# Last attention: scores and maxima contracted over one head's 32 rows, one head per row group

## The reference, cut to what matters

```python
x = x + _L1_attn_b_ref(_layernorm(x), W_qkv, b_qkv, W_o, b_o)

def _L1_attn_b_ref(x, W_qkv, b_qkv, W_o, b_o):        # 16 heads of 8, S = 1024
    Q, K, V = split(x @ W_qkv.T + b_qkv)              # each b, s, head, 8
    scores = einsum('bqhd,bkhd->bhqk', Q, K)
    scores = where(tril(ones(S, S)), scores, -inf)
    probs = softmax(scores / sqrt(8), axis=-1)
    return einsum('bkhd,bhqk->bqhd', V, probs).reshape(b, s, 128) @ W_o.T + b_o
```

## Time and profile before

| | us |
|---|---|
| three runs | 2196.89, 2202.60, 2202.69 |
| median | 2202.6 |
| span of the profiled execution | 2195.9 |
| last attention in it (1284 to 1959) | 675 |
| of this, units 1 to 14 (1372 to 1929.5) | 557.5, or 39.8 a unit |

### The profile page before, as it was taken

One profiled execution on the slowest core, in us unless ns is written; L12 is line 12 of the kernel. 1 busy time (PEld: TensorE's weight loads), 2 busy tenths in 40 slices (PEclk: granted clock), 3 DMA queues, 4 the chain that ended last, 5 costly groups with the idle time before them and its releaser, 6 DMA issues. The chain is left out here.

```text
span 2195.9 us, 35701 instructions
## 1 busy us (share of the span) xinstructions
PE 1937.5 (88%) x12178; PEld 1438.1 (65%) x12178; DVE 1695.5 (77%) x5509; ACT 1035.0 (47%) x1617; POOL 492.2 (22%) x558
## 2 busy tenths in 40 slices
PE   5886799998999967673799979999999999989999
PEld 3554699986899923332799965555555555549998
DVE  6997788876888879998688877766767767738887
ACT  3442244433444434442444444666666665554443
POOL 1110100012000022230200024534544543330000
PEclk8998999999999988876899989999999999999999
DMA  3000100000000010000000000000000000000000
GB/s 100 6 5 4 56 1 1 1 1 1 1 1 1 1 40 1 0 1 0 1 1 1 1 1 1 1 1 1 1 1 1 1 1 1 1 1 11 11 9 13
DMA packets 17638, 15.73 MB, mean 7 GB/s; under 512 B 4209, under 2 KB 16177, under 8 KB 16946
## 3 DMA queue, kind: packets, MB, share of 16 engines
q1 hardware_dynamic: 15152, 12.66, 1.8%
q10 hardware_dynamic: 2306, 0.78, 0.2%
HBM read 10.55 MB, written 2.88 MB: 6 GB/s over the span
## 5 line engine op out<-in xcount | busy, mean ns | idle before, releaser
L2205 ACT ACTIVATE soft_prob<-psum 128x1024 f32<-128x1024 f32 (+3 forms) x384 | 302.4, 812 | 203.8 <-PE psum L2085 202.2
L2297 DVE TENSOR_REDUCE soft_mx<-psum 128x1 f32<-128x512 f32 (+2 forms) x352 | 231.0, 688 | 116.1 <-PE psum L2155 79.3
L2155 PE MATMUL psum<-soft_own,soft_stack 128*128 128x512 f32 (+3 forms) x768 | 249.3, 376 | 24.5 <-DVE soft_mx L2293 10.7
L163 POOL TENSOR_TENSOR norm_rstd<-norm_mv,s_const_minus_half 128x4 f32<-128x4 f32 x64 | 65.2, 1019 | 915.0 <-DVE norm_mv L158 908.4
L2085 PE MATMUL psum<-soft_stack,soft_own 128*128 128x512 f32 (+3 forms) x768 | 225.4, 377 | 2.8 <-POOL soft_stack L2062 2.2
L2085 PEld LDWEIGHTS psum<-soft_stack,soft_own 128*128 128x128 f32 x768 | 125.3, 189 | 133.2 <-issue 81.6
L2293 DVE CUSTOM_DVE_ANT_0 psum<-psum,s_soft_sel 128x384 f32<-128x384 f32 (+1 forms) x256 | 157.4, 639 | 64.8 <-PE psum L2155 64.0
L2155 PEld LDWEIGHTS psum<-soft_own,soft_stack 128*128 128x128 f32 x768 | 139.8, 193 | 92.7 <-DVE soft_mx L2297 42.9
L1075 DVE SCALAR_TENSOR_TENSOR x<-psum,ffn1b_cw,x 128x128 f32<-128x128 f32 x512 | 144.1, 344 | 29.7 <-PE psum L949 20.9
L2102 PE MATMUL psum<-soft_prob,soft_v_pad 128*32 128x512 f32 (+3 forms) x1536 | 163.6, 498 | 3.5 <-ACT soft_prob L2205 2.1
L1075 DVE SCALAR_TENSOR_TENSOR x<-psum,ffn1a_cw,x 128x128 f32<-128x128 f32 x512 | 144.2, 344 | 27.2 <-PE psum L949 18.1
(11 more groups left out here) (381 smaller groups left out, 4114.0 us busy)
## 6 DMA issues: line engine op xcount, KB each, us to landing
s_ffn_w<-in_ffn_w SPq DMA_DIRECT2D x4, 1024.0 KB, 7.8
out_x<-x SPq DMA_DIRECT2D x8, 256.0 KB, 2.3
x<-in_x SPq DMA_DIRECT2D x4, 384.0 KB, 8.0
mamba_coef_dram<-mamba_out_coef SPq DMA_DIRECT2D x8, 96.0 KB, 1.6
s_ret_w<-in_ret_w SPq DMA_DIRECT2D x1, 640.0 KB, 3.5
x<-in_x SPq DMA_DIRECT2D x4, 128.0 KB, 3.5
s_ret_cos<-in_ret_cos SPq DMA_DIRECT2D x1, 512.0 KB, 7.0
s_ret_sin<-in_ret_sin SPq DMA_DIRECT2D x1, 512.0 KB, 7.3
```

Source lines behind the costliest of these rows:

```text
L163: self.nc.gpsimd.tensor_tensor(self.rstd[:, :], self.mv[:, :, 1], self.const["minus_half"][:, 0:GT], ALU.pow).then_inc(self.rstd_ready, 1)
L2155: ins = pe.matmul(per_head[:, n, :], stack[:, u % HT, i * P:(i + 1) * P], own[:, u % 3, g, half * BLK:half * BLK + width], start=(n == 0), ...
L2205: nc.scalar.activation(prob[:, done % PROBS, :, low(n):BLK], e_ps[:, n % 2, :, low(n):BLK], ACT.Exp, scale=float(HD) ** -0.5).then_inc(exp ...
L2297: nc.vector.tensor_reduce(mx[:, i, half, heads.start:heads.stop], bank[:, 0:width * len(heads)].rearrange("p (g k) -> p g k", k=width), AX ...
```

## The change

Scores and maxima contract over one head's 32 partitions and name their row group by `tile_position=(32 * g, 0)`. The masked copies `own`, their events, `ident` and `causal` are gone, and `keys` is kept for four units instead of two. A maxima job is always one head: 48 jobs a unit, and DVE adds the mask in all blocks of the diagonal (widths 128 to 512). Jobs come two per step, heads 2 and 3 in even steps and 0 and 1 in odd ones, where the scores of the step are of heads 0 and 1, and 2 and 3.

```diff
 def max_jobs():
         for half in range(1 + i // GT):
             width = min(BLK, (i + 1) * P - half * BLK)
-            heads = BLK // width
-            jobs += [(i, half, width, range(g, g + heads)) for g in range(0, HT, heads)]
+            jobs += [(i, half, width, g) for g in (2, 3, 0, 1)]
...
-            slots = [n for n in range(E_STEPS) for _ in range(2 if n % 2 or n % 8 == 0 else 1)]
             for j in range(M_JOBS):
-                at[slots[j * len(slots) // M_JOBS]].append(("m", u + 1, j))
+                at[j * E_STEPS // M_JOBS].append(("m", u + 1, j))
...
-            put((9, ("own", u + 2, 0)), (16, ("own", u + 2, 1)))
...
+        def head(g):
+            return slice(VW * g, VW * (g + 1))
...
 def scores(u, n):
                 for j in range(2):
-                    ins = pe.matmul(e_ps[:, n % 2, j, low(n):BLK], own[:, u % 3, 2 * pair + j, kt * P:(kt + 1) * P],
-                                    stack[:, u % HT, qb * BLK + low(n):(qb + 1) * BLK], start=True, stop=True)
+                    g = 2 * pair + j
+                    ins = pe.matmul(e_ps[:, n % 2, j, low(n):BLK], keys[head(g), u % HT, kt * P:(kt + 1) * P],
+                                    stack[head(g), u % HT, qb * BLK + low(n):(qb + 1) * BLK], start=True, stop=True,
+                                    tile_position=(VW * g, 0))
...
 kind == "m", PE
-                    for n, g in enumerate(heads):
-                        ins = pe.matmul(per_head[:, n, :], stack[:, u % HT, i * P:(i + 1) * P], own[...], ...)
-                    if half == i // GT and len(heads) > 1:
-                        ins = pe.matmul(per_head[:, :, width - P:width], ident[:, :], causal[...], ...)
-                    ins.then_inc(m_ready, 1)
+                    pe.matmul(bank[:, 0:width], stack[head(g), u % HT, i * P:(i + 1) * P],
+                              keys[head(g), u % HT, half * BLK:half * BLK + width], start=True, stop=True,
+                              tile_position=(VW * g, 0)).then_inc(m_ready, 1)
...
 kind == "st", ACT
-                    if i == 0 and b > 0:
+                    if b > 0:
                         act.wait_ge(score_ready, E_STEPS * (u - HT + 1))
-                    if i == 1 and u >= 2:
-                        act.wait_ge(*((own_first, 2) if u == 2 else (own_ready, 2 * (u - 2))))
...
 kind == "m", DVE
-                    if half == i // GT and len(heads) == 1:
+                    if half == i // GT:
                         nc.vector.tensor_tensor_reduce(bank[:, 0:width], bank[:, 0:width], mask_row[:, BLK - width:BLK],
-                                                       ..., mx[:, i, half, heads.start:heads.stop]).then_inc(m_done, 1)
+                                                       ..., mx[:, i, half, g:g + 1]).then_inc(m_done, 1)
                     else:
-                        nc.vector.tensor_reduce(mx[:, i, half, heads.start:heads.stop], bank[...] per head, AX.X, ALU.max)
+                        nc.vector.tensor_reduce(mx[:, i, half, g:g + 1], bank[:, 0:width], AX.X, ALU.max)
```

More of the change, by code:

```diff
@@ L1858, in softmax_events @@
     start = [("pad", 0), ("stat", 1), ("scale", 1), ("qk", 0, 1), ("qk", 0, 0)]
-    start += [first[0], ("own", 0, 0), ("v", 0), first[1]]
+    start += [first[0], ("v", 0), first[1]]
     start += [("xt", 1)] + maxima(0, 4) + [("qk", 1, 1)] + maxima(4, 8) + [("qk", 1, 0)] + maxima(8, M_FIRST)
-    start += [first[2], ("v", 1), second[0], ("sh", 0, 0), first[3], ("own", 0, 1)]
+    start += [first[2], ("v", 1), second[0], ("sh", 0, 0), first[3]]
     units = []
@@ L1877, in softmax_events @@
                 at[FIRST_STEPS + (j - 6) * (E_STEPS - FIRST_STEPS) // (M_JOBS - 6)].append(("m", 1, j))
-            put(*zip((1, 3, 4), second[1:]), (1, ("own", 1, 0)), (4, ("own", 1, 1)))
+            put(*zip((1, 3, 4), second[1:]))
             put((5, ("bias", 0)), (6, ("bias", 1)))
             put((9, ("oev", 0, 0)), *zip((10, 11, 13, 14), stack_events(0, 2)), (12, ("otr", 0, 0)), (15, ("sh", 1, 0)),
-                (12, ("own", 2, 0)), (16, ("own", 2, 1)), *zip((17, 18, 20, 21), stack_events(0, 3)), (19, ("pad", 1)))
+                *zip((17, 18, 20, 21), stack_events(0, 3)), (19, ("pad", 1)))
             units.append(at)
@@ L1908, in softmax_events @@
             put(*zip((15, 18), output_events(b)[0:2]))
-        if u + 2 < UNITS:
-            put((9, ("own", u + 2, 0)), (16, ("own", u + 2, 1)))
         units.append(at)
@@ L1936, in softmax_stage @@
         sel = sb("sel", [P, HT, 2, 2, P], F32R)
-        ident = sb("ident", [P, P], F32R)
-        causal = sb("causal", [P, P], F32R)
         full = sb("full", [P, BLK])
@@ L1941, in softmax_stage @@
         stack = sb("stack", [P, HT, SEQ], F32R)
-        keys = sb("keys", [P, 2, SEQ], F32R)
+        keys = sb("keys", [P, HT, SEQ], F32R)
         v_pad = sb("v_pad", [P, 2, TPB, HEADS, VW])
         prob = sb("prob", [P, PROBS, 2, BLK])
-        own = sb("own", [P, 3, HT, SEQ], F32R)
         mx = sb("mx", [P, TPB, 2, HT])
@@ L1955, in softmax_stage @@
         mask_ready = sem("mask_ready")
-        own_first, own_ready, top_ready = sem("own_first"), sem("own_ready"), sem("top_ready")
+        top_ready = sem("top_ready")
         sel_ready, pads_set, ones_set = sem("sel_ready"), sem("pads_set"), sem("ones_set")
@@ L2036, in event @@
                         nc.gpsimd.tensor_copy(mask_row[:, BLK - P:BLK], w["causal"][:, :]).then_inc(mask_ready, 1)
[L2037 to L2043, removed]
                 if kind == "stat":
@@ L2143, in event @@
                     u, j = at
-                    i, half, width, heads = MJOBS[j]
+                    i, half, width, g = MJOBS[j]
                     bank, back = m_bank(u, j)
                     if j in (0, M_FIRST):
-                        p = int(j > 0)
                         for part in range(2):
-                            pe.wait_ge(*freed("st", *divmod(u, HT), part, p))
-                        pe.wait_ge(*((own_first, p + 1) if u == 0 else (own_ready, 2 * (u - 1) + p + 1)))
+                            pe.wait_ge(*freed("st", *divmod(u, HT), part, int(j > 0)))
                     if M_JOBS * u + j >= back:
                         pe.wait_ge(m_done, M_JOBS * u + j + 1 - back)
-                    per_head = bank[:, 0:width * len(heads)].rearrange("p (g k) -> p g k", k=width)
-                    for n, g in enumerate(heads):
-                        ins = pe.matmul(per_head[:, n, :], stack[:, u % HT, i * P:(i + 1) * P],
-                                        own[:, u % 3, g, half * BLK:half * BLK + width],
-                                        start=(n == 0), stop=half != i // GT or len(heads) == 1)
-                    if half == i // GT and len(heads) > 1:
-                        ins = pe.matmul(per_head[:, :, width - P:width], ident[:, :],
-                                        causal[:, :].unsqueeze(1).to_broadcast([P, len(heads), P]),
-                                        start=False, stop=True)
-                    ins.then_inc(m_ready, 1)
+                    pe.matmul(bank[:, 0:width], stack[head(g), u % HT, i * P:(i + 1) * P],
+                              keys[head(g), u % HT, half * BLK:half * BLK + width], start=True, stop=True,
+                              tile_position=(VW * g, 0)).then_inc(m_ready, 1)
                 if kind == "sh":
@@ L2193, in _ @@
             act.wait_ge(*loaded)
-            nc.scalar.copy(ident[:, :], const["ident"][:, :])
-            nc.scalar.copy(causal[:, :], w["causal"][:, :])
             for t in range(HT):
@@ L2223, in event @@
                     u, now = HT * b + t, slice(p * BLK, (p + 1) * BLK)
-                    if i == 0 and b > 0:
+                    if b > 0:
                         act.wait_ge(score_ready, E_STEPS * (u - HT + 1))
-                    if i == 1 and u >= 2:
-                        act.wait_ge(*((own_first, 2) if u == 2 else (own_ready, 2 * (u - 2))))
-                    nc.scalar.activation(stack[:, t, now] if i == 0 else keys[:, u % 2, now], ps[:, :, :], ACT.Identity,
+                    nc.scalar.activation((stack if i == 0 else keys)[:, t, now], ps[:, :, :], ACT.Identity,
                                          bias=w["shift_rows"][:, i:i + 1]).then_inc(used, 1)
@@ L2294, in event @@
                                                        1.0, -3.0e38, ALU.add, ALU.max,
-                                                       mx[:, i, half, heads.start:heads.stop]).then_inc(m_done, 1)
+                                                       mx[:, i, half, g:g + 1]).then_inc(m_done, 1)
                     else:
-                        nc.vector.tensor_reduce(mx[:, i, half, heads.start:heads.stop],
-                                                bank[:, 0:width * len(heads)].rearrange("p (g k) -> p g k", k=width),
-                                                AX.X, ALU.max).then_inc(m_done, 1)
```

(2 more changed lines are left out.)

## The result

The changed kernel takes 2370.0 us (median of 4 runs, 2366.95 to 2382.34), the kernel before 2202.6 beside it: a ratio of 1.078 (95% interval 1.075 to 1.081), where 2189 was forecast. First the page of the changed kernel: span, then TensorE's busy tenths and granted clock in 40 slices of 59 us.

The account below looks back on a forecast made before the run. A ring through values, scores, maxima matmul, VectorE and bank was taken to bound the kernel. Terms -4 - 8 - 2 - 3 + 3 = -14 took the median of 2202.6 to 2189 us, range 2145 to 2235 (8 in 10).

Parts of the forecast that it names:

- the rival of the clock: TensorE streams less, idles more and its clock falls in the last attention: 2290 us in the mean, chance 0.12.
- V: Time of the values in a pair of steps: 1.00 us at 512 columns, 0.36 at 128, 9.42 a unit.
- c: Maxima load to VectorE's start: 0.54 us at 512 columns, then 0.48, 0.43 and 0.37 in narrower blocks.
- e: Last maxima load to the next values: 0.43 us at 512 columns, then 0.38, 0.32 and 0.27 in narrower blocks.
- The ring as costed: Loop of values, scores, maxima, VectorE and bank in the last attention: 36.9 us a unit against 37.2, chance 0.57.
- s: First score load to maxima load in a pair of steps: 0.05 us, replacing 0.56.
- D: Two maxima jobs on VectorE: 1.29 us for reduces; with masks 1.41, 1.16, 0.91 and 0.66 from 512 to 128 columns.
- that rival: Row groups of scores and maxima don't run together: 2275 us, or 2218 with loads one at a time; chance 0.16.
- the -14: Whole effect forecast in us: fourteen units -4, key copies -8, start -2, last unit -3, unit 0 +3.
- Key copies, -8: POOL's copy of step 16 no longer delays the triangles and the values after them: 0.6 us in each of 14 units.
- Start, last unit, unit 0: First copy gone from DVE at the start -2 us, shorter scores in the last unit -3, more VectorE jobs in unit 0 +3.
- Expected signs: Scores and maxima starting within 0.03 us, full-reduce pairs 3.3 to 3.4, clock 1.00 from 1372; wrong if clock under 0.95.

Follow-up runs that it names:

- e1: Changed kernel, but scores and maxima contract over all 128 rows with unmasked keys and no row groups: 2233.0 us, ratio 1.015 to the kernel before.
- e2: Changed kernel, but scores and maxima of every head use the 32 rows of head 0, heads 1 to 3 left out: 2628.0 us, ratio 1.192.
- e8: Changed kernel plus matmuls with zeros on 256 columns behind the values of each pair of steps: 2328.2 us, ratio 1.057.
- e10: Kernel before, with the second half of the masked copies behind step 12 instead of 16: 2205.7 us, ratio 1.0027.
- e5: Changed kernel plus two products with zeros in TensorE's wait before the third maxima job of a pair of steps: 2305.3 us, ratio 1.043.
- e3: Changed kernel, but the scores alone contract over 128 rows, unmasked, while maxima keep row groups: 2416.0 us, ratio 1.098.
- e12: Kernel before with the new job list, and the first half of the masked copies behind step 12 instead of 9: 2280.2 us, ratio 1.035.

## Why the prediction was wrong

*What failed* is one sentence under the rival of the clock: that the new pauses "are short, and those before, of 0.5, didn't lower the clock of 1.00". It looked for what lowers the clock in TensorE's pauses. The runs put it in the rows: with the same two waits for VectorE in a pair and 128 rows the clock is 1.00 (e1), with hardly a pause and 32 rows 0.53 (e2). The sentences on V, c and e at half clock were right about the price, 1.3 a pair: the one pair shown at half clock is 1.46 longer, to its last row, than the one at full clock, and the mean of all pairs at half clock is 1.23 over the same places before (below). Only the chance, 12%, and the share of half clock behind the 2290 were wrong; all at half clock was priced at 2400, and 2370 at a mean of 0.64 lies near it. The rule cited there from the Trainium skill, "TensorE: Matmul & The Clock Gate", Part 1, that the clock follows how busy TensorE has been, fits only if busy is not read from the profile's share: 92% at 0.64, 99% at 0.53, 96% at 1.00.

*The ring as costed* was right, at full clock: V 0.99 for 1.00; s 0.01 for 0.05, as the Trainium skill, cited there, would have had it (0.12 to the second scores, whose row groups the maxima hold); c 0.56 for 0.54; D 1.29 for reduces as said, and with masks, to the end of the last read-out, 1.14 for 1.16 at 384 columns (1988.83 to 1989.97) and 0.87 for 0.91 at 256 (1982.09 to 1982.96); e 0.43 as said; the pair 3.34 for 3.36. One size was off: c in narrow blocks, 0.57 at 256 columns (1981.52 to 1982.09), not 0.43, and 0.57 at 128 (1557.92 to 1558.49), not 0.37, likely because narrow maxima run beside scores of 512 columns. Row groups do run together; that rival falls. Its price of 0.51 a pair was too high: it takes 0.56 to the maxima's matmul and then c from the maxima's load, which comes earlier. e1, where scores and maxima do go one behind the other, pays 0.33.

*What a unit would take at full clock* can be put together from pairs alone. 43 of the changed kernel's pairs behind unit 0 lie wholly at 1.00 and take 3.34 in the mean; the same places of a unit take 3.37 before and 3.67 in e1. 102 lie wholly at 0.50 and take 4.37; the same places take 3.14 before. So at full clock the change is worth 0.04 x 180 pairs, some 7 us: the -14 that was forecast, or none. This is an estimate, since 36 of the 43 lie in five of a unit's twelve places; e8 has pairs at 1.00 in all twelve, and in units 1 to 14 they, less their zeros (0.43, or 0.18 in the narrowest), give some 10. The 1.23 too much in 102 pairs is 125 us; unit 0 and the pairs that see both levels have the rest of the 169.

*Key copies, -8*: the delay is as read in the earlier trace rows, but it isn't in every unit. Without it (e10) a pair is 0.75 shorter in 4 units of 14, so 3 us and not 8. The removal of the copies does more in the new list, 41 us, by a collision that the kernel before avoids. *Start, last unit, unit 0*, at -2: the first values come 3.9 us earlier (1319.4 for 1323.3), but unit 0 is 24 us longer (83.7 for 60.1 between first exponentials), at a clock of 0.69 and less. *Expected signs*: starts together and pairs of 3.3 to 3.4 appeared; "PE clock 1.00 from 1372 on" didn't, and 0.64 lies under the 0.95 that was named as a sign of being wrong.

No run beat the kernel before. The filler can't: the twelve pairs of a unit at full clock, their means added, are 40.4 us in e5, longer than the 38.7 of before; e1 has 40.4 too, and would still need its keys masked.

## What to carry to other kernels

Matmuls on fewer rows are worth their saving only where TensorE's clock doesn't pay for it: look at the granted clock of the stretch that they are to run in, and cost the stretch at both levels, because a share of busy time in the profile doesn't tell rows. Price a saving on TensorE against what keeps the clock up: if the time saved turns into waiting for another engine, the work that was removed may have been holding the clock. Mixing tile forms inside a loop costs time at each turn, here 0.2 us (0.42 from load to load in e3, where the form changes, 0.23 within the pair of loads of e1), and so does a filler in another form.

## What the runs showed that was not expected

Adding work to the critical path made the kernel faster: 0.4 us of zeros in each pair of steps, 42 us less in all (e8). More clock went with more time in e3, by changes of form. And an event's step in POOL's order is no time: a copy put three steps later started at the same triangle (e12).
